# The quantised rows of a language-model layer: turned to channel-major by TensorE in every step

## The reference

```python
h = table[x] * keep_mask[x]                     # gathered rows, 32 x 512 x 256
# first sub-layer, on layernorm(h)
u, res = split(n1 @ in_proj_w.T)                # 512 and 256 wide
u = causal_conv4(u) + conv_b                    # depthwise, 4 taps along the tokens
g = u * sigmoid(softplus(u @ dt_proj_w.T + dt_proj_b))
y = scan(state = 0.9 * state + 0.1 * g)         # along the tokens
h = h + y @ out_proj_w.T + res
# second sub-layer, on layernorm(h)
q, scale = fp6_quantise(n2, blocks of 32)       # and the weight likewise
xd = q * scale
h = h + xd @ wd.T + ffn_bias
```

## Time and profile before

| | |
|---|---|
| device time, median of 3 (range) | 1170.4 us (1169.04 to 1170.95) |
| the profiled execution: span from first to last instruction | 1167.3 us |
| mean granted clock of TensorE in it | 0.934 |
| PE busy (matmul) | 1011.5 us, 87% |
| DVE busy | 1104.0 us, 95% |
| ACT busy | 582.0 us, 50% |
| POOL busy | 740.2 us, 63% |
| DMA moved | 68.32 MB, of it 51.08 MB on the hardware queue |

### The profile page before, as it was taken

How to read it: one execution, slowest core, us unless ns; L and a number is a source line. 1 busy time by engine, 2 the same in 40 slices (tenths; PEclk the granted TensorE clock), 3 DMA queues, 4 the chain that set the end, 5 groups by cost and what they waited for, 6 DMA issues and landing times.

```text
span 1167.3 us, 16219 instructions
## 1 busy us (share of the span) xinstructions
PE 1011.5 (87%) x5652; PEld 871.8 (75%) x5652; DVE 1104.0 (95%) x1627; ACT 582.0 (50%) x966; POOL 740.2 (63%) x521
## 2 busy tenths in 40 slices
PE   3789888889888889888889888899888899888887
PEld 2678777778777778777778777788777787777777
DVE  6879999999999999999999999999999999999995
ACT  4455445455445555444555454555454554454541
POOL 5556666676656676666676566676666675666562
PEclk9799999899989999998999899999989998999998
DMA  4001121112121112121211121211211121211111
GB/s 131 19 19 52 58 73 55 55 55 70 58 72 49 59 54 65 61 72 36 72 54 63 63 67 41 69 57 58 68 59 49 54 72 54 73 55 55 43 49 54
DMA packets 51470, 68.32 MB, mean 59 GB/s; under 512 B 10096, under 2 KB 42736, under 8 KB 51440
## 3 DMA queue, kind: packets, MB, share of 16 engines
q1 hardware_dynamic: 45296, 51.08, 13.4%
q0 software_dynamic: 6144, 16.85, 5.4%
HBM read 35.40 MB, written 32.51 MB: 58 GB/s over the span
## 4 chain that ended last, share of the span: by engine, by line
PE 73%; DVE 15%; issue 10%; ACT 1%; POOL 1%; DMA 0%; DVEq 0%; ACTq 0%; POOLq 0%
PE psZ L960 9%; PE psZ L961 9%; PE psZ L967 9%; PE psU L918 7%; PE psU L914 5%; PE psU L915 5%; PE psO L940 3%; PE psO L941 3%; PE psO L942 3%; DVE nT_lo L811 3%; DVE u L649 3%; PE psO L932 3%; PE psT L1027 2%; PE psO L934 2%; PE psO L1015 2%
## 5 line engine op out<-in xcount | busy, mean ns | idle before, releaser
L649 DVE SCALAR_TENSOR_TENSOR u<-psU,cw,u 128x511 f32<-128x511 f32 x378 | 265.2, 740 | 16.2 <-ACT u L436 11.7
L350 POOL TENSOR_TENSOR y_lo<-y,y_hi 128x512 fp32r<-128x512 f32 x128 | 163.2, 1287 | 180.8 <-ACT y_hi L456 180.1
L357 POOL TENSOR_TENSOR u_lo<-u,u_hi 128x512 fp32r<-128x512 f32 x128 | 189.9, 1483 | 115.5 <-ACT u_hi L443 107.2
L744 DVE TENSOR_TENSOR_SCAN y<-decay,g 128x512 f32<-128x512 f32 x128 | 231.2, 1806 | 3.4
L918 PE MATMUL psU<-nT_lo,in_hi 128*128 128x512 f32 x252 | 127.2, 505 | 121.1 <-DVE nT_lo L811 121.1
L960 PE MATMUL psZ<-u_hi,dt_hi 128*128 128x512 f32 x512 | 203.7, 398 | 4.9 <-ACT u_hi L443 4.4
L961 PE MATMUL psZ<-u_hi,dt_lo 128*128 128x512 f32 x512 | 202.9, 396 | 0.0
L967 PE MATMUL psZ<-u_lo,dt_hi 128*128 128x512 f32 x512 | 197.6, 397 | 0.0
L335 POOL DMA_INDIRECT rows<-table,ids x128 | 149.9, 1171 | 35.3 <-issue 34.1
L918 PEld LDWEIGHTS psU<-nT_lo,in_hi 128*128 128x128 f32 x252 | 60.1, 238 | 149.2 <-DVE nT_lo L811 135.3
L436 ACT ACTIVATE u<-psU,cb,cw 128x512 f32<-128x512 f32 x126 | 97.7, 775 | 145.0 <-PE psU L918 145.0
(11 more groups left out here) (109 smaller groups left out, 2489.0 us busy)
## 6 DMA issues: line engine op xcount, KB each, us to landing
out<-h SPq DMA_DIRECT2D x31, 512.0 KB, 2.9
turned<-xb SPq DMA_DIRECT2D x30, 512.0 KB, 2.7
xT<-turned SPq DMA_DIRECT2D x120, 128.0 KB, 2.9
rows<-table,ids POOLq DMA_INDIRECT x128
y<-dt_wT SPq DMA_DIRECT2D x1, 1024.0 KB, 5.8
g<-in_wT SPq DMA_DIRECT2D x1, 768.0 KB
ids<-x SPq DMA_DIRECT2D x32, 2.0 KB, 2.6
ow_stage<-out_wT SPq DMA_DIRECT2D x1, 512.0 KB, 7.8
```

The lines of the kernel that those rows point to most:

```text
L350: pool.tensor_tensor(y_lo[:, m, :], y[:, m, :], f32(y_hi[:, m, :]), ALU.subtract).then_inc(y_lo_ready[m], 1)
L357: pool.tensor_tensor(u_lo[:, m, :], u[:, m, :], f32(u_hi[:, m, :]), ALU.subtract).then_inc(u_lo_ready[m], 1)
L649: dve.scalar_tensor_tensor(u[:, m, back:T], u_psum_tile(st, m)[:, 0:T - back], cw[:, m, TAPS - 1 - back:TAPS - back], u[:, m, back:T], ALU ...
L744: dve.tensor_tensor_scan(y[:, m, :], decay[:], g[:, m, :], 0.0, ALU.mult, ALU.add).then_inc(y_ready[m], 1)
```

## The change

In every step with a tail, `xd` is turned by TensorE (`transpose_xd`, eight 128 by 128 transposes) straight after `out_proj(1)`, into `psT`. ACT rounds the high part out of PSUM (placed between `split_u(2)` and `split_u(3)`), DVE subtracts the low part out of PSUM (`split_xT`, placed ahead of `add_h(0)`). Gone are the 32 by 32 block transposes on DVE, the write to and the reads from DRAM on SP's queue, POOL's low part, the tensors `xb` and `xT`, and the block order of n2. `psT` now serves two users in a step: the transposes of xd wait until n1's low part was split (`nT_lo_ready`), the transposes of n1 wait until xd's was (`xT_lo_ready`).

```diff
@@ semaphores and helpers @@
         def turned_by_pe(s, part):
-            return s - (NSEQ - 2) + 1 + (part or 0)
+            return s + 1 + (part or 0)
@@ SP @@
-                if st.tail and st.main:
-                    sp.wait_ge(xb_ready, s - 1)
-                    sp.dma_start(turned, xb[:]).then_inc(turned_written, 16)
-                    sp.wait_ge(turned_written, 16 * (s - 1))
-                    for q in range(Q):
-                        blocks = turned.rearrange("(a j) (q n) -> q j a n", a=Q, q=Q)[q]
-                        sp.dma_start(xT[q * BLOCK:(q + 1) * BLOCK, :].rearrange("j (a n) -> j a n", a=Q),
-                                     blocks).then_inc(xT_loaded, 16)
@@ POOL, after inverse_root1 @@
-                if st.tail and st.main:
-                    pool.wait_ge(xT_hi_ready, s - 1)
-                    pool.tensor_tensor(by_token(xT_lo), xT_by_token, f32(by_token(xT_hi)),
-                                       ALU.subtract).then_inc(xT_lo_ready, 1)
@@ ACT, split_xT @@
-                    if st.main:
-                        act.wait_ge(xT_loaded, Q * 16 * (s - 1))
-                        act.activation(by_token(xT_hi), xT_by_token, ACT.Copy).then_inc(xT_hi_ready, 1)
-                        return
@@ ACT, order @@
                 if st.main:
                     split_u(2)
+                if st.tail and st.main:
+                    split_xT()
+                if st.main:
                     split_u(3)
                     tanh(0)
-                if st.tail and st.main:
-                    split_xT()
-                if st.main:
                     tanh(1)
@@ DVE, inverse_scale @@
-                    if not st.main:
+                    if later(s - 1) and st.tail:
                         dve.wait_ge(t2_psum, turned_by_pe(s - 2, None))
@@ DVE, order @@
                 if st.tail:
                     dequantise(None, own=False)
-                    dve.wait_ge(xd_ready, s - 1)
-                    if later(s - 2):
-                        dve.wait_ge(turned_written, 16 * (s - 2))
-                    dve.transpose(xb[:], flat(xd[:])).then_inc(xb_ready, 1)
                 if st.main:
                     convolve(2, 2, 3, 2, 3, 3)
+                if st.tail:
+                    split_xT(None)
                 if st.back:
                     add_h(0)
                     add_h(1)
@@ PE, transpose_xd @@
+                    if st.main:
+                        pe.wait_ge(nT_lo_ready, s + 1)
                     to_channels(lambda c, k: xd[:, c, k * P:(k + 1) * P], xd_psum(part), t2_psum, part)
@@ PE, order @@
                 if st.back:
                     out_proj(1)
-                if st.tail and not st.main:
+                if st.tail:
                     for part in st.tail_parts:
                         transpose_xd(part)
                 if st.main:
                     dt_proj_0_1()
@@ PE, before n1's transposes @@
+                    if st.tail:
+                        pe.wait_ge(xT_lo_ready, s - 1)
```

More of the change, by code:

```diff
@@ L107, in lm_tower_kernel @@
         xd = sb("xd", [P, C, D])
-        xb = sb("xb", [P, C * D])
-        xT = sb("xT", [P, C * D])
         xT_hi, xT_lo = sb("xT_hi", [P, KD, T], F32R), sb("xT_lo", [P, KD, T], F32R)
@@ L128, in lm_tower_kernel @@
         fd = xd[:, 0:KD, :]
-        Q = P // BLOCK
-        n2_blocks = n2[:].rearrange("p c d -> p (c d)").rearrange("p (q k c j) -> p k q c j", q=Q, k=KD, c=C)
-        xT_by_token = xT[:].rearrange("p (a m i) -> p m a i", a=Q, i=BLOCK)
         psT = psum("psT", [P, KD, T])
@@ L187, in lm_tower_kernel @@
             sem(n) for n in ("amax_ready", "bscale_ready", "brecip_ready", "q_ready", "xd_ready", "t2_psum"))
-        xb_ready = sem("xb_ready")
-        turned_written, xT_loaded = sem("turned_written"), sem("xT_loaded")
         xT_hi_ready, xT_lo_ready = sem("xT_hi_ready"), sem("xT_lo_ready")
@@ L197, in flat @@
             return ap.rearrange("p k t -> p (k t)")
-        def by_token(xT_part):
-            return flat(xT_part[:]).rearrange("p (m a i) -> p m a i", a=Q, i=BLOCK)
         def later(v):
@@ L221, in __init__ @@
                 self.second = known and s == 1
-                self.by_block = not known or s - 1 < NSEQ - 2
                 self.back_parts = (0, 1) if known and s - 1 == NSEQ - 1 else (None,)
@@ L487, in normalise2 @@
                     for c in range(C)[span(part)]:
[L488 to L493, removed]
+                        ins = act.activation(n2[:, c, :], h2[:, nb, c, :], ACT.Identity, bias=nmr2[:, c:c + 1],
                                              scale=rstd2[:, c:c + 1])
@@ L532, in step @@
                     split_u(2)
-                    split_u(3)
-                    tanh(0)
                 if st.tail and st.main:
@@ L537, in step @@
                 if st.main:
+                    split_u(3)
+                    tanh(0)
                     tanh(1)
```

## The result

The changed kernel takes 1235.1 us (median of 4, 1233.9 to 1237.0) against 1170.7: 1.055 times as long, 95% interval 1.0536 to 1.0567. The profiled execution, one of 1236.1 us, has a span of 1234.2 us and a mean granted clock of 0.911; before, they were 1167.3 and 0.934.

What follows compares the result with a forecast made beforehand. Each step was taken as PE alone to add_h, then DVE alone to nT_lo. Trip +3.6 less 2.04 gave +1.57 short, +1.7 long; between +48 and +77 us, +64 was taken: 1234 us, range 1198 to 1250.

Steps and rivals of the forecast that it cites:

- DVE's block transpose and the DRAM trip: Transpose lies on DVE before add_h, beside PE; nobody waits for the DRAM reads and writes; removing both is worth 0.
- `mean_term1` gives back 2.04 us a step: On DVE after add_h: without POOL's low part its stall goes, 2.04 us gained per step, bounds 0 to 2.15.
- The new trip: After out_proj(1): PE transposes, ACT's high part, DVE's split_xT, all ahead of add_h; 3.6 to 3.7 us later per step.
- The u_lo delay: u's high part queues behind xT's on ACT, making POOL's u_lo half a microsecond late; only the 4.2 us bound has it reach the gate.
- `scan(2)` keeps its stall: On DVE: POOL's last gather again meets q, so y_lo still stalls scan(2) by 2.58 us; change 0, bound -2.58.
- Rival (a): POOL's y_lo waits and scan(2) does not: about 34.1 us a step, 1139 us, range 1133 to 1169; chance 0.12.
- Rival (b): DVE is the bound and the trip hidden, so the 2.04 us is pure gain: 1109 us; chance 0.04.
- rival (c): Slower, but part given back by smaller y stalls or less time at the low clock: 1155 to 1200; chance 0.08.
- Long steps: Steps with PE's slower first piece (16.50 us against 15.28), 36.00 us before, 37.7 after; expected to be the more frequent.
- today's mix: The present share of short and long steps, about three in four short; with it the change costs 48 us.
- the lost cover: DVE reaches split_xT 2 us or more before it can run, so every slow matmul in PE's first piece shows in full.
- the short step: Step of 34.89 us: PE alone for 15.28 us up to add_h, then DVE alone to nT_lo; 36.45 us after.

Runs made afterwards that it cites:

- The two experiments on POOL's subtraction: Changed kernel with a 128x1024 GpSimd subtraction put back: 1260.1 us; kernel before with GpSimd's low part of xT moved behind the four gathers: 1168.1 us.
- moving the split: Changed kernel with y_lo begun only after scan(2), 1102.4 us; the same with split_xT moved from ahead of add_h to behind statistics2, 1023.6 us.
- the experiment that settles the order by a wait: Changed kernel with one wait on GpSimd, so that y_lo begins only when scan(2) is done: 1102.4 us, ratio 0.942.
- The two runs with fillers: Twelve 128x512 throwaway matmuls added where PE waits at each step's end: changed kernel 1167.2 us, kernel before 1162.4 us.

## Why the prediction was right

1234 us were predicted and 1235.1 measured, and the mechanism was the one named. That the two agree to 1 us is partly chance, as the last step below shows. Step by step:

- *DVE's block transpose and the DRAM trip are worth nothing.* Right: with the transpose gone, DVE waits for the taps instead (69.4 us at L610), and no wait names the DRAM trip in either kernel. It holds while PE's clock falls. With the clock held, DVE alone sets the step of the kernel before, and the block transpose lies in its way: by my estimate for about 1.0 us a step, as PE is done that much before `add_h` there.
- *`mean_term1` gives back 2.04 us a step.* Right: 2.30 to 0.14, start to start 2.22 to 0.06, so 2.16. The two experiments on POOL's subtraction show its cause; that it read as two operands in SBUF against a GpSimd instruction was the right reading.
- *The new trip costs 3.6 to 3.7 us a step ahead of `add_h`.* Right in length: `add_h` starts 3.27 us after out_proj(1) ends; before, it started 0.3 to 0.45 us ahead of that end. That it stands on the path is shown by moving the split (1102 to 1024 with `scan(2)` short and the clock up in both).
- *The u_lo delay stays off the path.* Right: 13.6 us of weight loads waiting, in 33 pieces of at most 0.6, ahead of a gate that comes later anyway.
- *`scan(2)` keeps its stall, because the last gather again meets `q`.* Right: 3.80, with the same 0.21 us. Rival (a) was only a question of order, and the experiment that settles the order by a wait shows its price: 1102, not the 1139 that I gave it. I had left PE's clock as it was. Rival (b), the hidden trip, needed DVE to come late to its split, and DVE stands 2.49 us there. Nothing of rival (c) came: the `scan(2)` stall kept its length, and the clock was low for longer, not for less.
- *Long steps become more frequent.* Right in direction, mis-sized: 64 us over 30 steps stands for some two long ones in three, and it is all 28 of the middle steps, 37.5 us. They lose 2.32 us each against the 35.22 that the same steps took before, where the sum had 2.13, but they are 28 and not 30. On the span that makes 66.9 us, not 64. The median came out nearer because the launch stood less over the span than before (1.9 us, not 3.1), and the profiled execution was 1 us above the median: small errors against each other.

What I did not see was how far the clock carried the loss. The sum put 48 us on "today's mix" and only the rest on the clock. The two runs with fillers say it the other way round: with the clock held the change costs 5 us. Both are true of different baselines: the 48 are counted from steps whose slow matmuls were already partly on the path, and the trip then puts the rest there. The prediction had the sentence on the lost cover, but gave it 16 us. And it read the short step as PE's alone up to `add_h`, while DVE came to it only 0.28 us before PE: with the clock held, DVE is the later of the two.

## What to carry to other kernels

Before work is moved between engines, lay one step out in time and mark on each engine which pieces run alone: a new hand-over in such a piece costs its length, less what the engine was late anyway, however much busy time it removes; and two places later in the same list, where its input is just ready, the wait is gone. Look at instructions that are longer than others of their form and see what GpSimd does beside them; one wait that puts GpSimd's work beside a PSUM-reading instruction was worth 100 us here. And where TensorE waits some 4 us in every step and its work behind the wait has no cover, shortening the wait gains more than its length, as its clock then stays at the upper level (4.8 us a step for a stall of 2.6).

## What the runs showed of the hardware

- A wait of PE of 3.9 to 4.0 us in a step went with granted clock 0.50 behind it, for 3.4 or about 6 us. With waits of 3.2 us the mean clock was 0.938, with waits of 0.64, 1.35, 1.44 or, with fillers, some 1.2 to 1.3 us it was 0.985 to 0.990. The Trainium skill, "TensorE: Matmul & The Clock Gate", section "HAM oscillation — how this bites in real kernels", describes a matmul loop in which the wait of each round sends the clock down, so that every round starts slow; the trace agrees (0.50 behind each wait of 4.0 us).
- A DVE instruction that reads two SBUF operands stands still while a GpSimd subtraction in SBUF runs: 2.30 for 0.14 us, 3.80 and 6.11 for 1.22 us. Those with a PSUM operand (`nT_lo` at 1.20 beside `y_lo`) do not.
- An addition with one SBUF operand and a constant, 128x4, was stopped too (1.30 for 0.17 us).
- Where GpSimd's subtraction follows a gather directly, it goes first although the DVE instruction's recorded start is 0.21 us earlier. Why is open; only that it repeats in each step was seen.
